# A fused tokenizer, linear attention and mixture-of-experts kernel: the hand-kept instruction orders of all five engines replaced by another set

## What is computed

```python
h = einsum('bhid,oi,od->bho', x, weighted_sum, weight)      # x: 4 x 512 x 256 x 4, 8 MB
h = concatenate([h, txt], axis=1)                           # 4 images of 512 + 32 tokens, 256 wide
h = h + attn(layernorm(h))     # gated linear attention, 16 heads of 16, a decay per channel
h = h + ffn(layernorm(h))      # top-2 of 8 experts, capacity ceil(T*K*1.25/E) = 680, 256 -> 1024 -> 256
```

## Time and profile before

| | |
|---|---|
| median of 3 runs | 623.98 us (622.28 to 625.66) |
| the profiled execution | 622.14 us |
| its span, first to last instruction | 620.4 us |
| granted TensorE clock, mean | 0.962 |
| PE busy | 577.8 us (93%) |
| DVE, ACT, POOL busy | 393.8, 334.7, 309.0 us |
| DMA | 59.88 MB, mean 97 GB/s |

### The profile page before, as it was taken

One profiled execution on the slowest core, in us unless ns is written; L12 is line 12 of the kernel. 1 busy time (PEld: TensorE's weight loads), 2 busy tenths in 40 slices (PEclk: granted clock), 3 DMA queues, 4 the chain that ended last, 5 costly groups with the idle time before them and its releaser, 6 DMA issues.

```text
span 620.4 us, 14064 instructions
## 1 busy us (share of the span) xinstructions
PE 577.8 (93%) x4940; PEld 540.7 (87%) x4940; DVE 393.8 (63%) x1031; ACT 334.7 (54%) x891; POOL 309.0 (50%) x370
## 2 busy tenths in 40 slices
...
GB/s 204 270 315 116 2 52 52 41 52 78 28 131 20 98 19 48 1 103 86 200 119 154 24 256 31 99 182 8 221 68 51 221 17 180 109 30 103 23 2 48
DMA packets 44874, 59.88 MB, mean 97 GB/s; under 512 B 5184, under 2 KB 33424, under 8 KB 44816
## 3 DMA queue, kind: packets, MB, share of 16 engines
q1 hardware_dynamic: 37136, 49.28, 25.9%
...
## 4 chain that ended last, share of the span: by engine, by line
PE 83%; DVE 10%; issue 3%; ACT 2%; DVEq 0%; DMA 0%; POOL 0%; SPq 0%; ACTq 0%; POOLq 0%
PE ps L1936 48%; PE ps L1983 15%; PE ps L2173 3%; PE ps L2118 3%; PE ps L1978 3%; PE ps L2159 2%; PE ps L2062 2%; PE ps L2154 2%; PE ps L1957 1%; PE ps L2134 1%; PE ps L2166 1%; DVE sb_lg L1766 1%; DVE sb_att L1703 1%; PE ps L2080 1%; DVE sb_bn L1541 1%
## 5 line engine op out<-in xcount | busy, mean ns | idle before, releaser
L1936 PE MATMUL ps<-sb_xe_hi,sb_rounded 128*128 128x256 f32 (+1 forms) x1024 | 207.5, 297 | 2.4 <-DVE sb_xe_lo L1896 2.4
L1936 PEld LDWEIGHTS ps<-sb_xe_hi,sb_rounded 128*128 128x128 f32 x1024 | 166.6, 190 | 2.7 <-DVE sb_xe_lo L1896 2.7
L1936 PE MATMUL ps<-sb_xe_lo,sb_rounded 128*128 128x320 f32 (+1 forms) x512 | 151.7, 296 | 0.0
L1936 PEld LDWEIGHTS ps<-sb_xe_lo,sb_rounded 128*128 128x128 f32 x512 | 97.0, 189 | 0.0
L1983 PE MATMUL ps<-sb_rounded,sb_h_hi 128*128 128x256 f32 x512 | 94.5, 286 | 0.0
L1425 DVE TENSOR_TENSOR sb_dec<-ps,sb_gate 128x256 f32<-128x256 f32 (+1 forms) x121 | 55.2, 456 | 57.6 <-ACT sb_gate L1127 54.8
L1127 ACT ACTIVATE sb_gate<-ps 128x256 f32<-128x256 f32 (+1 forms) x121 | 49.1, 406 | 67.4 <-PE ps L1936 66.5
L1983 PEld LDWEIGHTS ps<-sb_rounded,sb_h_hi 128*128 128x128 f32 x512 | 78.3, 188 | 0.0
L973 POOL DMA_INDIRECT out_rows<-sb_att,sb_s_token x40 | 61.8, 1545 | 29.9 <-DVE sb_att L1436 23.1
L1983 PE MATMUL ps<-sb_rounded,sb_h_lo 128*128 128x256 f32 x256 | 71.9, 281 | 0.0
L1455 DVE TENSOR_TENSOR sb_h_lo<-sb_dec,sb_h_hi 128x256 fp32r<-128x256 f32 x128 | 70.2, 548 | 1.9 <-ACT sb_h_hi L1390 1.1
...
## 6 DMA issues: line engine op xcount, KB each, us to landing
sb_x_in<-in_x SPq DMA_DIRECT2D x16, 512.0 KB, 4.8
sb_raw<-in_L_ffn_W SPq DMA_DIRECT2D x16, 512.0 KB
sb_x_in<-in_L_ffn_W SPq DMA_DIRECT2D x16, 512.0 KB, 4.5
xe_rows<-sb_xr SPq DMA_DIRECT2D x3, 1457.5 KB, 15.1
...
sb_xn<-in_L_ffn_W SPq DMA_DIRECT2D x8, 512.0 KB, 4.3
sb_h<-in_L_ffn_W SPq DMA_DIRECT2D x8, 512.0 KB, 4.8
out_rows<-sb_h SPq DMA_DIRECT2D x16, 128.0 KB, 1.7
```

The source lines that it names most:

```text
L1936: ins = pe.matmul(out_ap, lhs, rhs, start=(first and i == 0), stop=(last and i == n - 1))
```

## The change

Only the five strings change. The same steps run on the same engines with the same arithmetic; two lines fewer of text shift all line numbers by two (L1936 becomes L1934). The SyncE string and the head and the end of two others:

```diff
 SP_ORDER = """
-tok_load.1 tok_load.0 load_x.0.1 load_x.0.0 load_txt.0 last_load w5_load load_x.0.2 decay_load load_x.0.3
-rows_init.0 load_txt.1 load_x.1.0 rows_init.3 load_x.1.1 load_w13.0 rows_init.2 load_x.1.2 zero_rows.0
-rows_init.1 load_x.1.3 load_x.2.0 load_x.2.1 load_x.2.3 out.0.0 out.0.2 load_x.2.2 out.0.1 out.0.3 out.0.4
+load_txt.0 tok_load.1 load_txt.1 tok_load.0 load_x.0.0 load_x.0.1 last_load w5_load rows_init.3 rows_init.2
+rows_init.0 decay_load rows_init.1 zero_rows.0 load_x.0.2 load_x.0.3 load_w13.0 load_x.1.0 load_x.1.1 load_x.1.2
+load_x.1.3 load_x.2.0 load_x.2.1 load_x.2.3 out.0.0 load_x.2.2 out.0.1 out.0.2 load_x.3.0 out.0.4 out.0.3 load_txt.2
...
 PE_ORDER = """
-we_turn.0@4 we_turn.1@5 we_turn.2@6 we_turn.3@7 x_turn.0.0.0@4 x_turn.0.1.0@5 x_turn.0.0.1@0 x_turn.0.1.1@6
-embed.0.0@7 embed.0.1@4 x_turn.0.2.0@5 x_turn.0.2.1@6 g1_turn@7 x_turn.0.3.1@1 x_turn.0.3.0@2 embed.0.2@5
+we_turn.0@4 we_turn.3@5 we_turn.2@6 x_turn.0.0.1@7 we_turn.1@4 x_turn.0.1.1@5 x_turn.0.0.0@6 route.0@4
+x_turn.0.1.0@7 embed.0.0@6 embed.0.1@4 route.1@7 route.2@5 g1_turn@6 g1_mul@7 xn_turn.0.1@4 xn_turn.0.0@5
+v_proj.0.1@6 x_turn.0.2.1@4 xn_turn.0.4@5 v_proj.0.0@7 x_turn.0.2.0@6 x_turn.0.3.1@5 x_turn.0.3.0@4 embed.0.2@6
...
-attn_out.3.2@6 head_norm.3.3@4 head_norm.3.4@5 attn_out.3.4@6 attn_out.3.3@5 rank.3@7 early_turn.0@6 rank.4@5
-counts@4 early_turn.1@7 early_turn.2@6 early_up.0@6 early_up.2@2 early_up.1@4 early_up.5@6 early_up.3@4 early_up.4@0
+head_norm.3.3@5 attn_out.3.4@6 attn_out.3.3@4 rank.3@7 early_turn.2@5 early_turn.0@6 early_turn.1@4 rank.4@7
+counts@5 early_up.0@0 early_up.1@2 early_up.3@6 early_up.2@4 early_up.5@0 early_up.4@2 early_up.6@6
...
 DVE_ORDER = """
-ln2_stats.3.3 shift.3 ln2_newton.3.1 router.3.3 router.3.4 weigh.3 slots.3 top2.4 limits.4 shift.4 counts
-early_turn.0 weigh.4 slots.4 early_turn.1 early_turn.2 early_up.0 early_split.0 early_up.1 early_up.2 early_split.1
+ln2_stats.3.4 ln2_stats.3.3 slots.3 ln2_newton.3.1 router.3.3 router.3.4 top2.4 shift.4 limits.4 early_turn.2
+early_turn.0 early_turn.1 weigh.4 slots.4 counts early_up.0 early_up.1 early_split.0 early_split.1 early_up.3
```

More of the change, by code:

```diff
@@ L54 @@
[L54 to L68, removed]
```

212 lines of the change are left out of this document (112 added, 100 removed).

## The result

The changed kernel takes 630.6 us, the median of 4 runs (628.55 to 631.84); the kernel before, on the same chip and in the same rounds, 624.0 (622.28 to 625.66). The ratio is 1.0098, 95% interval 1.0068 to 1.0129: 6.6 us slower by the medians, where 14.1 were forecast. The profiled execution took 628.55 us with a span of 626.8, so it lies 2.1 us under the median; that of before lay 1.9 under its own.

A forecast was written before the change was run, and what follows sets the result against it. TensorE was taken to bound the kernel from 20 us on, fed by a queue with nothing to spare. Lag +14.4, clock +2.1 and routing -2.4 sum to +14.1 us: 638 us forecast, 8-in-10 range 628 to 645.

The forecast's parts named there:

- SyncE's order: Start, SyncE's queue: four blank transfers ahead of tile 0.2 make it land at 39.0 us, bounds 35.7 to 40.9.
- How far TensorE is behind: TensorE at tile 0.2: 17.4 us of work, formerly done by 24.6 us, so a lag of 14.4 us, 11.1 to 16.3.
- The clock: TensorE after the wait: it resumes at the low clock level, one loss of +2.1 us, bound none to two.
- The end of the routing: Before the first early up product: three turns ahead of weigh.4 and slots.4 remove a 2.37 us wait, -2.4, bounds -3 to 0.
- Everything else: Orders and banks of the images' steps: no wait seen to appear or go, 0 us, within -6 to +6.
- Loads not held: Rival at the start: tiles get through beside the blank rows, no lag, about 619 us (616 to 622); chance 0.11.
- New orders that stall: Rival across the orders: newly given banks make TensorE wait, +8 us on top, about 646 us; chance 0.05.
- The lag taken back: Rival after the start: later waits shrink and 10 us come back, ending at 628 us (624 to 630); chance 0.09.
- Tile 0.2 between 36 and 41: Sign at SyncE's queue: tile 0.2 lands at 36 to 41 us behind four blank transfers.
- Some 17 us of work in 39: Sign at the start: TensorE does some 17 us of work in the first 39 us.
- The wait at L2048: Sign at g1_turn: TensorE waits there for the decay weights until about 31 us.
- A long wait at L2060: Sign at tile 0.2's turn: TensorE shows a second long wait there, for tile 0.2 to land.

The follow-up runs named there:

- c_blanks_last: The changed kernel with its blank transfers moved behind tile 1.2, decay weights behind tile 0.2 and zero rows ahead of tile 1.0: 619.6 us, ratio 0.9932.
- f_c_old_turns: c_blanks_last with the end of the routing in the order of the kernel before, on all engines: 622.4 us, ratio 1.0001.
- b_blanks_first: The kernel before with the changed kernel's first part of SyncE's order, four blank transfers ahead of tile 0.2: 650.8 us, ratio 1.0437.
- h_decay_first: The changed kernel with the decay weights' loads ahead of all four blank transfers: 630.3 us, ratio 1.0128.
- d: The changed kernel with two of its four blank transfers ahead of tile 0.2, the other two behind tile 0.3: 623.8 us, ratio 1.0031.
- g: The kernel before with the changed kernel's end of the routing, including the order and banks of the early up products: 617.3 us, ratio 0.9912.

## Why the prediction was right about the sign and wrong about the size

The experiments split the 0.98% into three, by the ratios, since the kernels ran in different rounds (the spans given are worked out from the two intervals):

| term | forecast | measured | from |
|---|---|---|---|
| blank rows ahead of tile 0.2 | +16.5 (lag 14.4, clock 2.1) | +10.4, within 2.4 | after less c_blanks_last, 1.0098 - 0.9932 |
| end of the routing | -2.4 | -4.3, within 2.4 | c_blanks_last less f_c_old_turns, 0.9932 - 1.0001; 4.2 in the timelines |
| all other orders and banks | 0 | +0.1, within 1.9 | f_c_old_turns to before, 1.0001 |
| sum | +14.1 | +6.1 (6.6 by the medians) | |

*SyncE's order* held: tile 0.2 landed at 39.4 us for 39.0, the decay weights at 32.3 for 31.5, in order of issue. That it came to within 0.4 us is partly luck: in b_blanks_first the same queue landed the tile at 35.95, near the lower bound of 35.7. I also had completion out of order taking perhaps 1.2 us off. What the Trainium skill (DMA: Bandwidth & Descriptors, Queues, rings and completion order) says there is narrower than I took it: a transfer's completion on one DMA engine lands only after every earlier write of that engine, and its example of an overtaking is a later transfer on a single engine beside an earlier one on all 16. The landings of the zero rows at 38.3 and of the tile at 39.4 give no sign of an overtaking.

*How far TensorE is behind* is **the step that failed**. The 17.4 us of work were counted about right: c has done 17.69 when it reaches tile 0.2, the last 1.5 of them at the low clock. But I set them against the progress of the old order: "The kernel before had done 12.8 us by 20 us and was dense after, so it had done 17.4 by 24.6 us." The row for that window of the kernel before bears the reading out:

```profile
0.00:24.60 24.60, 17.41 (x133) 16.83 (x134) 13.82 (x33) 13.96 (x28) 9.61 (x33) 1.00 0.82 232
```

The comparison has to be with the new order with its loads on time, and c_blanks_last is that kernel: it is there at 27.43, 2.8 us later. Of the 2.8 us, 1.0 is the later first instruction (7.83 for 6.83), which the prediction named as the price once nothing hides it, and some 1.5 are the idle times of the chain of small steps, which waits for ScalarE and VectorE 0.4 to 0.5 us each time; the rest is work. All of it lies ahead of the point where the wait for the tile begins, so the wait hides it: in h_decay_first TensorE comes to stand at 27.42. Over the whole kernel the delay brings no loss that can be seen: f's total is that of the kernel before. Which later steps of the new order make up for it wasn't looked into.

*The clock* added nothing here. I added 2.1 us for a resume at the low level. The changed kernel does run at the low clock behind the wait (0.57 and 0.92 in the windows), but from tile 0.2 on so does c_blanks_last without a wait (0.50 from 26 to 32 us): the product of 264 columns with `sb_xn_lo` takes 0.42 us in both. Ahead of tile 0.2 it does not: `g1_turn` to `v_proj.0.1` take 5.0 us in c and 6.8 in the changed kernel, and that is hidden only because the tile lands no earlier. Against c the difference at tile 0.2 is 39.44 - 27.43 = 12.0 us, and at the first `range_sum` it is 78.33 - 66.28 = 12.05. Nothing comes on top. That holds for this order and not in general: b, whose order is at 1.00 there when nothing is late, loses 6.1 us to the low clock behind its two waits, and d 1.6. So 16.5 + 0.4 (landing) - 2.8 (baseline) - 2.1 (clock) = 12.0, of which 11.0 arrive in the medians. Where the last microsecond went isn't settled; it is within what the runs scatter.

*The end of the routing* had the right mechanism and little more than half the size. I took off the one wait that the profile names, 2.37 us, and left the two turns behind `counts` on the path; they too moved under the wait for `limits.4`. The chain from L1826 to the first early up product measures 7.33 us against 3.14 in g. My bound of -3 was too narrow for what the new turns can save; in the changed kernel's own profile, with 4.3, it is just met.

*Everything else*, taken as 0 within 6 either way, measured +0.1 within 1.9.

**The rivals.** Loads not held: refuted by the landing at 39.4. New orders that stall: refuted by f. The lag taken back (628) came closest in time, but for another reason: b still has 29.7 us at the experts' start (26.8 at the end by the medians), h and the changed kernel keep most of theirs against c (9.9 and 12.0 us at the first `range_sum`, 9.2 and 7.9 at the experts in these single executions, that of the changed kernel lying 2.1 us under its median and c's 0.8 above). In these two executions the difference falls from 12.0 us at the second `range_sum` to 7.5 at the fourth; in h, the same measure stays at 9.3 or more. So against the kernel without the hole little or nothing was taken back (11.0 of 12.0 us arrive by the medians, 10.4 by the ratios, both within the scatter of 12.0); the lag was smaller from the start.

**The signs.** Tile 0.2 between 36 and 41: yes. Some 17 us of work in 39: 20.06 by 39.44 us, where c needs 17.69 for the same steps; the rest is the lower clock (0.79 over that stretch for 0.96), which makes the same steps longer and here costs nothing, as it lies ahead of the tile's landing. The wait at L2048 until about 31: until 32.4. A long wait at L2060: no, 0.22 us only. By the prediction's own prices the small steps behind the decay weights (0.6 + 1.1 + 1.2 + 0.75 = 3.65 us) would have left a wait of 3.9 us; they took 6.8, at the low clock and with idle times of 0.5 us between them. The sentence that I would be wrong if the experts' start moved by less than 6 us though tile 0.2 landed late came true at 5.9.
